# Moving the exponentials of the third score bank into the tile's own step

## The reference

```python
# attention: latents = layernorm(x), context = ctx_1024
q = q * (1.0 + scale[:, None, :, None]) + shift[:, None, :, None]
qk = jnp.einsum('bihd,bjhd->bhij', q, k) * attn_scale      # 1024 tokens x 77 rows x 16 heads
attn = jax.nn.softmax(qk, axis=-1)
out = jnp.einsum('bhij,bjhd->bihd', attn, v)
x = x + out.reshape(b, -1, INNER) @ Wout
# experts: router softmax over 9, top 2, then
gate = silu(xn @ Wg); hidden = gate * (xn @ Wu); out = hidden @ Wd      # weighted by the router
```

## Time and profile before

| | |
|---|---|
| Median of 3 runs | 819.4 us (818.67 to 820.06) |
| The profiled execution, its own time | 818.16 us |
| Its span, first to last instruction | 816.4 us |
| TensorE busy | 790.7 us (97%) |
| VectorE busy | 663.6 us (81%) |
| ScalarE busy | 618.7 us (76%) |
| GpSimd busy | 374.7 us (46%) |
| Mean granted TensorE clock | 0.992 |

### The profile page before, as it was taken

The page is one execution under the profiler, slowest core; times in us unless marked ns, Lnnn a source line. Parts: engine busy times, 40 slices in busy tenths (PEclk is TensorE's granted clock), DMA queues, the critical chain, the costliest instruction groups (busy, mean ns, idle before and its releaser), DMA issues.

```text
span 816.4 us, 19726 instructions
## 1 busy us (share of the span) xinstructions
PE 790.7 (97%) x6021; PEld 753.8 (92%) x6021; DVE 663.6 (81%) x1620; ACT 618.7 (76%) x1958; POOL 374.7 (46%) x534
## 2 busy tenths in 40 slices
PE   7999999999999999998999999999999999999994
PEld 6966999999999999888999999999999999999994
DVE  6677888888889888889678888788887878878782
ACT  5578898889889888744677777677786877778762
POOL 1021387688778767772323333333433333333343
PEclk9999999999999999999999999999999999999997
DMA  8275801401310020636475273465656546383222
GB/s 298 68 178 146 259 27 38 146 28 40 121 57 34 28 92 28 202 110 183 101 218 136 52 217 83 100 145 144 182 150 161 145 143 164 82 228 79 46 23 31
DMA packets 78060, 96.14 MB, mean 118 GB/s; under 512 B 10695, under 2 KB 65155, under 8 KB 77955
## 3 DMA queue, kind: packets, MB, share of 16 engines
q1 hardware_dynamic: 64515, 76.98, 30.6%
q0 software_dynamic: 13440, 17.90, 12.4%
HBM read 109.19 MB, written 30.23 MB: 171 GB/s over the span
## 4 chain that ended last, share of the span: by engine, by line
PE 87%; DVE 4%; ACT 3%; DVEq 1%; issue 1%; DMA 1%; POOL 1%; SPq 1%; POOLq 0%
PE banks L351 25%; PE banks L352 24%; PE banks L353 24%; PE banks L1418 4%; PE banks L1398 2%; PE banks L1584 2%; PE banks L1432 2%; ACT prob L1091 1%; DVEq L1637 1%; PE banks L1372 1%; PE banks L1346 1%; PE banks L1384 1%; DMA tok<-expert_in 1%; DMA wkv_sb<-in_L_xattn_Wkv 1%; PE banks L1556 0%
## 5 line engine op out<-in xcount | busy, mean ns | idle before, releaser
L351 PE MATMUL banks<-tok_t_hi,wgt_hi 128*128 128x256 f32 x704 | 202.4, 287 | 1.9 <-issue 1.6
L353 PE MATMUL banks<-tok_t_hi,wgt_lo 128*128 128x256 f32 x704 | 198.1, 281 | 0.0
L352 PE MATMUL banks<-tok_t_lo,wgt_hi 128*128 128x256 f32 x704 | 198.0, 281 | 0.0
L991 POOL DMA_INDIRECT result<-res,tok_id x72 | 121.0, 1681 | 167.0 <-ACT res L1226 145.0
L1091 ACT ACTIVATE prob<-banks,row_min 128x77 f32<-128x77 f32 x512 | 161.5, 374 | 2.3 <-DVE row_min L1804 2.3
L351 PEld LDWEIGHTS banks<-tok_t_hi,wgt_hi 128*128 128x128 f32 x704 | 134.6, 191 | 3.9 <-issue 3.9
L352 PEld LDWEIGHTS banks<-tok_t_lo,wgt_hi 128*128 128x128 f32 x704 | 134.2, 191 | 0.0
L353 PEld LDWEIGHTS banks<-tok_t_hi,wgt_lo 128*128 128x128 f32 x704 | 133.9, 190 | 0.0
L1091 ACT ACTIVATION_READ_ACCUMULATOR prob<-banks,row_min 128x1 f32 x512 | 130.6, 257 | 0.0
L351 PE MATMUL banks<-wgt_hi,hid_hi 128*128 128x256 f32 x360 | 102.1, 284 | 0.6 <-DVE hid_hi L2120 0.6
L352 PE MATMUL banks<-wgt_lo,hid_hi 128*128 128x256 f32 x360 | 101.3, 281 | 0.0
(11 more groups left out here) (274 smaller groups left out, 2206.3 us busy)
## 6 DMA issues: line engine op xcount, KB each, us to landing
wgt<-in_L_ffn_Wg SPq DMA_DIRECT2D x29, 704.0 KB
wgt<-in_L_ffn_Wu SPq DMA_DIRECT2D x29, 640.0 KB
wgt<-in_L_ffn_Wd SPq DMA_DIRECT2D x29, 640.0 KB
tok<-expert_in SPq DMA_DIRECT2D x32, 258.0 KB, 3.7
spare_wgt<-in_L_ffn_Wg SPq DMA_DIRECT2D x9, 704.0 KB, 4.3
spare_wgt<-in_L_ffn_Wu SPq DMA_DIRECT2D x9, 640.0 KB, 6.0
spare_wgt<-in_L_ffn_Wd SPq DMA_DIRECT2D x9, 640.0 KB, 6.1
valmat_f<-valmat_dram SPq DMA_DIRECT2D x4, 1197.0 KB, 6.3
```

What stands on the lines that cost most here:

```text
L351: nc.tensor.matmul(to, a[0], b[0], start=first, stop=False)
L352: nc.tensor.matmul(to, a[0], b[1], start=False, stop=False)
L353: return nc.tensor.matmul(to, a[1], b[0], start=False, stop=last)
L991: nc.gpsimd.indirect_dma_start(out, bass.IndirectOffsetOnAxis(ap=tok_id[:, t % NOTES, a:a + 1], axis=0), res[i][:, a, :], None, compute_op ...
```

## The change

ScalarE made the exponentials of bank 2 one step late: at the head of step s, behind the first two rounds, it did bank 2 of tile s - 1. Only in step 0 did it do them in the tile's own step. With the change it does them in the tile's own step always, right behind bank 1's. No other engine's order changes, and no semaphore or wait is added or taken away; the waits move with the instructions.

```diff
@@ ScalarE's step(s, c)
                 if s == T + 1:
                     nc.scalar.activation(row_sum[0][:, 1:2], eps[:], ACT.Silu)
-                if has(s, 1) and s > 1:
-                    softmax_exp(s - 1, c - 1, 2)
                 if has(s, -1):
                     normed_plus_one(s + 1, (c + 1) % 2)
...
                 if has(s, 0):
                     softmax_exp(s, c, 1)
-                if not s:
+                if has(s, 0):
                     softmax_exp(s, c, 2)
```

## The result

The changed kernel takes 820.03 us (median of 12 runs, 818.8 to 822.15), the kernel before on the same chip 818.75 us (12 runs): ratio 1.0018, 95% interval 1.0011 to 1.0026. That is 1.3 us slower, just under the 0.2% that the prediction called no change. The forecast was +1.3 us, from 819.4 to 820.7 us; the base of 819.4 was the median of three runs and lies 0.65 us over that of twelve, so the measured time is 0.67 us under the forecast. The difference came out as predicted, but in the loop several of its terms were not where the prediction had put them, and their errors cancelled.

The account below looks back on a forecast made before the run. TensorE, busy 97% of the span and losing only 0.7 us in the loop, was taken as the bound. +0.37 - 0.33 + 0.54 + 0.25 + 0.44 + 0.05 = +1.3 us on 819.4 gave 820.7 us, range 819.0 to 823.3.

Parts of the forecast that it names:

- The plain step: Twenty-odd ordinary loop steps: ScalarE's idle 1.33 us shrinks to 0.3, TensorE sees nothing, cost 0.
- The ring: Loop chain from ScalarE's rounds through VectorE's minima to ten heads and back: 8.2 us against 8.53.
- The start: Steps 1 and 2: moved heads delay ScalarE's roundings by 1.20 us, TensorE's third scores net +0.37 us.
- Steps 4 to 7: Of a batch: value matrix rounding fits the gap before the minima, VectorE no longer held up, -0.33 us.
- Step 7: First batch's boundary: later x_off from GpSimd delays picks, 9.28 us instead of 8.74, +0.54 us.
- The boundaries: Batch ends: heads behind ScalarE's wait for x_off make the next step's rounds late, +0.8 and twice +0.2 us.
- slack of 0.65: Plain step: picks done at 7.76, wanted at about 8.45, so TensorE has 0.65 us behind a late ScalarE.
- Two sides share their memory access: VectorE's 0.43 us idle before picks at 122.22 agrees with SBUF contention with GpSimd, without proving it.
- 2 (the slack swallows it): VectorE catches up, only the start is paid and step 6 won: 819.4 + 0.05, no change; chance 0.17.
- 5 (faster): VectorE no longer held up, the loop's 0.7 us come back, boundaries cost nothing: 818.7 to 819; chance 0.06.
- 3: Slower by ScalarE's cycle: decides from 0.3 us more per step, 2.8 us per 0.1 beyond; chance 0.14.
- Rival 4: VectorE and GpSimd collide at the boundaries, four steps at 0.4 us each, 1.6 us more: 822.3; chance 0.08.

Follow-up runs that it names:

- own_01: The kernel before, with only tiles 0 and 1 making the third bank in their own step, later tiles a step later: 818.94 us, ratio 1.0005.
- own_but_1_last: The kernel before, with all tiles making the third bank in their own step except tile 1 and the last of each batch: 818.80 us, ratio 0.9999.
- picks_first_after: The changed kernel with pick and picks put ahead of xn on VectorE: 819.91 us, ratio to the kernel before 1.0018.
- own_but_last: The kernel before, with all tiles making the third bank in their own step except the last of each batch (7, 15, 23, 31): 819.53 us, ratio 1.0013.
- shift_after: The changed kernel with 21 tiny memsets more on VectorE, seven in each of steps 9 to 11: 820.34 us, ratio to the kernel before 1.0019.
- pad_after: The changed kernel with two small copies on ScalarE behind gap_exp in each of steps 3 to 31: 822.97 us, ratio to the kernel before 1.0053.

## Why the prediction was right, and where it was not

**The plain step** was right in each number. The ring of 8.2 us measured 8.13, and its play is what kept 20-odd steps at 8.53.

**The start**, +0.37, measured +0.43, and own_01 shows it alone. The wait for the residual, which the prediction moved by 1.20 us, shows in TensorE's row of step 2. It stands 4.91 us into the step, and 3.70 in the kernel before:

```profile
83.80 0.44 PE L1416 MATMUL banks<-ident,prob 128*128 128x128 f32 x2 [1.31 <-DVE prob_t_lo L1777]
```

**Steps 4 to 7** failed: "VectorE is no longer held up, and the 0.33 us of the earlier trace rows should go". own_but_1_last, where ScalarE is on time, gains 0.07 us of them. The rest was never ScalarE's: it is VectorE's pause ahead of `picks`, without which step 14, with the same work, loses nothing. In place of the gain, steps 5 and 6 lost 0.39 us: GpSimd's late division held xn, and `picks` behind it.

**Step 7** failed as a place. The prediction had GpSimd late by 0.6 us at `x_off` and let nothing of that be felt before step 7. The division of step 4, which it had late by 0.78 us, was late by 0.91 (102.48 - 101.28, less 0.29 by which the loop begins later), and `x_off` by 0.81 (zn from 126.36 to 127.46, less 0.29), but its late division had held xn, and with it `picks`, in steps 5 and 6 already, so that TensorE reached step 7 late by the same 0.81 us (123.65 - 122.55 - 0.29) and found `x_off` at its old 3.81 us, which the prediction had named as a sign of being wrong. picks_first_after removes that hold and gets the loss in step 7, 9.01 us where the prediction had 9.28. Start and first batch up to step 7 sum to +0.82 measured and +0.58 predicted. That the two come so near is luck: steps 5 and 6 were off by +0.72 us and step 7 by -0.54.

**The boundaries** failed in size. Behind them the rounds come 0.73 us late (1.40 instead of 0.67), where the prediction had about 1.0: it ended ScalarE's step with gap_exp's full 0.42 us, but with work waiting the next instruction starts 0.18 us behind gap_exp's start (167.67 and 167.85 above). 0.73 is hardly over the slack of 0.65, and at step 24 it is 0.52, so step 24 loses nothing and step 8 0.17. Step 16 has VectorE's pause of 0.42 besides: 0.73 + 0.42 - 0.65 = 0.50, measured 0.49. The prediction had no such term. own_but_last takes away the first and brings step 16 back to 8.53 us. shift_after takes away the second and 0.17 us of the first, and the step takes 8.54 us; by the same sum the pause alone would still have cost 0.56 + 0.42 - 0.65 = 0.33 us. That the rounds are later at step 16 than at step 24 is probably the work of the pause of step 13, which makes `x_off` late and which shift_after moves as well; that isn't shown by itself. Steps 8, 16 and 24 together were predicted at +0.69 and measured +0.66, again by errors that cancel.

**"Two sides share their memory access"** was right of the chip and wrong of the row. The pause in the earlier trace rows is no collision: it stands at the 320th instruction of VectorE in every kernel whose order up to there is the same, and the others at distances of 128 or 256 from it, in shift_after too, where other work stands there. The collision is at another instruction, xn, which shows no idle time at all, only a longer duration.

**The rivals**: 2 (the slack swallows it) and 5 (faster) did not come, nor did 3: pad_after shows that it needed 0.40 us more in the ring. Rival 4, collisions between VectorE and GpSimd, did occur, but in steps 5 and 6 and not at the boundaries, and not as added pauses of 0.4 us.

## What to carry to other kernels

An instruction that is sometimes longer than its own minimum, with no wait ahead of it, is held by something that the waits don't name: compare its end with the ends of what another engine does beside it. A pause with no releaser may belong to its place in the queue: count the instructions, those that the views leave out too. Work that is put behind a wait (the heads behind `x_off`) costs its whole length at that wait, even where the engine has idle time in every other step; leaving the old order in those few steps brought the 1.3 us back. Before a ring is filled, its length should be weighed against the period: the last 0.4 us of play cost nothing in any plain step and 2.9 us in the kernel, by what could no longer be caught up with.

## What the runs showed of the hardware

- VectorE's xn (fp32, one tensor in, 128 x 256, both in SBUF) can't end while GpSimd's 128 x 1232 product runs: 0.40 us alone, 0.88, 1.05, 1.47, 1.88 and 2.31 us beside it, always ending at least 0.14 us behind it. `pick` (fp32, two tensors in, both in SBUF) is held too, 0.42 us beside it in picks_first_after. GpSimd's instruction isn't slowed (2.24 to 2.27 us in all).
- VectorE pauses for up to 0.46 us at fixed places of its stream: 123.32, 179.52, 207.83, 234.60 and 291.27 in the changed kernel, the same instructions in the kernel before. They are 256, 128, 128 and 256 instructions apart, drains, semaphore and register instructions counted. The Trainium skill (Runtime: NRT & Kernel Launch, Instruction fetch mechanics) has each engine fetch its instructions in blocks of 256 and calls the cost of a boundary mostly hidden. The trace differs: the distances are multiples of 128, half such a block, and the pauses of steps 6 and 16 cost TensorE time. No run shows that they are fetches.
- On ScalarE the next instruction starts 0.18 or 0.19 us behind the start of a 128 x 1 gap_exp whose row says 0.40 us.
